# A fused layer-norm, graph and aggregation kernel: 14 pairs of batches multiplied by the weight in stage 1 in place of 8

## Chip, cores and metric

One core of one Trainium2 chip. The metric is the device time of one execution in microseconds (us). The kernel before took 948.14 us, the median of three runs (946.9 to 948.69).

## What is computed

x is 64 batches of 128 x 1024 numbers (f32), the weight ("adj") 128 x 128, the bias 128 numbers, gumbel 1024 x 1024 x 2. Cut to what matters:

```python
h = relu(layernorm(x, axis=-1))                    # rstd and shift of each row
xp = transpose(h, (2, 0, 1))                       # n=1024 nodes, 64 batches, 128
x_avg = xp.mean(axis=1); x_norm = x_avg / norm(x_avg)
sim = (x_norm @ x_norm.T + 1) * 0.5
adj = (sim + gumbel[:, 0] > 1 - sim + gumbel[:, 1])
nmask = clip(adj + adj.T + eye, 0, 1)
common = nmask @ nmask.T
W = adj * where(valid, common**2 / common.max(), 0)
Wn = dinv[:, None] * W * dinv[None, :]             # dinv = column sums ** -0.5
xw = einsum('nbt,to->nbo', xp, weight)
out = x + transpose(einsum('sd,sbt->dbt', Wn, xw) + bias, (1, 2, 0))
```

## The kernel before

The 64 batches are 32 pairs. Only after all of x has been read is the graph known, so the kernel reads x twice, and multiplies by Wn last.

**Stage 1** (to some 112 us of the span). SyncE loads the two batches of pair p into one of 8 places of xin (L316 to L321), and waits first until ScalarE has read the pair eight before. VectorE takes the statistics (long_step, L708, four instructions a pair), in groups of two pairs (GROUPS, L35), and turns those of one group into rstd and shift between the statistics of the next (L731 to L743). ScalarE takes the root that this needs (std, L481), applies norm and relu (relu, L487, two instructions a pair, into one of 4 places of h1), and copies products out of PSUM (keep, L499). The sum of h over all batches is shared: GpSimd adds the first batch of each pair to hsum (L433 to L436), TensorE adds the second through an identity into PSUM banks 0 and 1 (L1106 to L1112; of the last pair both batches). For 8 pairs, SPILLED, TensorE also multiplies the two batches by the weight (keep_product, L1097) into banks 2, 3 and 4, 5; a product may start once the copy of the same batch of the pair kept before is out. The 16 products stay in bmem (kept, L96).

**After x.** SyncE's queue has four loads of gumbel (1 MB each, load_gumbel, L326), the stores of the first four kept pairs to DRAM (spill_group, L311) between them, four more loads of gumbel, each behind a threshold, then the other four stores. Thresholds, gumbel 1 minus gumbel 0, take the place of kept products in bmem: VectorE makes rows 0 to 3 (threshold, L770), GpSimd rows 4 to 7 (L439). Row 0 stands ahead of the last addition to hsum (L776 to L780) in VectorE's order. TensorE takes two of four late batches times the weight (L1119, L1136), then sums of the squares over columns, VectorE from them the norms (L784), TensorE the 1024 x 1024 similarity row by row (L1148), VectorE compares it with the thresholds (L854). Transposes, counts of common neighbours and column sums follow. 

**Scaling and quad 0.** TensorE replicates the scale of the columns in banks 1 and 2 (L1131), ScalarE copies both to SBUF (L599 to L601), VectorE multiplies each half row of the graph by it (scaled, L907) and makes the differences that the multiplication wants (inner_of, L919).

**The quads.** Wn times xw is done for two pairs at a time, 16 quads (L1294 on), by two nested levels of seven products in place of eight: 7 slots of 28 matrix instructions in four banks each; the sums of the inputs are VectorE's (inner_sums, outer_sums), those of the outputs VectorE's, ScalarE's and GpSimd's (finish, add_kept, finish_kept; finish_here on GpSimd, L456). Quad 0 holds the two last pairs; quads 2 to 5 (LOADED) load the 8 kept pairs back from DRAM (L388 to L394). The other pairs are read from x again (load_h), put through norm and relu by ScalarE (relu_of, L534), multiplied in half batches of four matrix products ("chunks", weigh, L1235) and copied out by ScalarE (L587). This work is spread over the quad before by PLACES (L48): 12 chunks in quad 0 (for quad 1 and half of quad 6, called EXTRA; that half goes through DRAM, L407), 4 in quad 5, 8 in each of the quads 6 to 14; 88 in all. Of the chunks of quad 0, two come before the replication, four after it (FIRST_CHUNKS), six after slot 1. ScalarE's part of this, in its order: weigh(0, BEFORE), the two copies of the column scale, weigh(0, AFTER), where the third relu stands between the copies of chunks 3 and 4. Slot 0 may start once the first six are copied (L1277).

Semaphores order everything between engines; each engine runs its own list in order.

## Time and profile before

| | |
|---|---|
| median of three runs | 948.14 us |
| the profiled execution's own time | 950.07 us |
| its span | 948.2 us |
| busy: TensorE, VectorE, ScalarE, GpSimd | 909.9, 725.0, 352.1, 215.2 us |
| chain that ended last | 82% TensorE, 9% VectorE, 6% ScalarE |
| matrix products of the quads (L1311) | 690.4 us |
| chunks (L1246) | 91.8 us |
| products kept in stage 1 and the late ones (L1089) | 320 instructions |
| read from and written to DRAM | 108.07 and 42.99 MB |

Times in rows are microseconds from the span's start unless marked ns. PE is TensorE, PEld its weight loads, DVE VectorE, ACT ScalarE, POOL GpSimd, SP or SPq SyncE and its queue. A row of a timeline gives start, length, engine, line of the kernel, operation, what it writes and reads, how many instructions it merges, and in brackets the idle time before it with what ended it; the length of a merged row runs from the first start to the last end. Successive instructions overlap a little, so that the distance of two starts is shorter than a length. The profiled execution's own time is 1.9 us longer than its span.

### The profile page before, as it was taken

To read this page: it belongs to the slowest core of one execution; us is meant where nothing else is said; L and a number is where in the kernel's file an instruction comes from. 1 tells how busy PE (TensorE), PEld (TensorE's weight loads), DVE (VectorE), ACT (ScalarE), POOL (GpSimd) and SP (SyncE) were. 2 spreads that over 40 slices of the span, in tenths; PEclk is the share of its full clock that TensorE was granted. 3 is DMA by queue.
4 is the path that set the end of the run, shared out by engine and by line. 5 is a ranking of instruction groups with operands and counts; after the bars stand their busy time and mean duration, and the time that the engine had idled before them with its cause. 6 is when DMAs were issued, how large, how long until landed. Compare 5 with 4: busy or idle time off the path is not lost.

```text
span 948.2 us, 12421 instructions
## 1 busy us (share of the span) xinstructions
PE 909.9 (96%) x4603; PEld 770.4 (81%) x4607; DVE 725.0 (76%) x1492; ACT 352.1 (37%) x565; POOL 215.2 (23%) x178
## 2 busy tenths in 40 slices
PE   3899999798999999999999999999999999999997
PEld 2655565787888888888888988888889888888886
DVE  7899568999978879786858676758586766767687
ACT  4799818542212121223233423342424342424130
POOL 3588533102211111130201111111111111111111
PEclk9899999999999999999999999999999999999999
DMA  9999981321706244361524333241524242424022
GB/s 361 350 347 376 389 316 59 156 89 45 260 25 249 86 181 141 125 199 67 176 91 149 118 115 153 94 173 67 192 76 178 89 178 89 178 76 169 34 101 89
DMA packets 37485, 151.88 MB, mean 160 GB/s; under 512 B 3376, under 2 KB 3504, under 8 KB 34224
## 3 DMA queue, kind: packets, MB, share of 16 engines
q1 hardware_dynamic: 37424, 151.07, 43.3%
q8 instruction: 37, 0.61, 0.2%
q14 instruction: 24, 0.20, 0.1%
HBM read 108.07 MB, written 42.99 MB: 159 GB/s over the span
## 4 chain that ended last, share of the span: by engine, by line
PE 82%; DVE 9%; ACT 6%; issue 2%; DMA 0%; DVEq 0%; ACTq 0%
PE ps L1311 67%; PE ps L1246 7%; ACT main L495 4%; DVE bmem L915 3%; DVE stats L712 2%; PE ps L1089 2%; PE ps L1167 2%; PE ps L1148 1%; ACT bmem L502 1%; DVE bmem L908 1%; PE ps L1108 1%; PE ps L1224 1%; DVE main L1026 0%; DVE bmem L927 0%; ACT half_std L484 0%
## 5 line engine op out<-in xcount | busy, mean ns | idle before, releaser
L1311 PE MATMUL ps<-bmem,main 128*128 128x256 f32 x3136 | 690.4, 379 | 7.4 <-DVE main L993 3.8
L1311 PEld LDWEIGHTS ps<-bmem,main 128*128 128x128 f32 x3136 | 589.7, 190 | 85.2 <-issue 5.5
L463 POOL TENSOR_TENSOR main<-main 128x256 f32<-128x256 f32 x32 | 27.5, 859 | 533.0 <-ACT main L621 477.2
L993 DVE TENSOR_TENSOR main<-ps,main 128x512 f32<-128x512 f32 x124 | 76.5, 623 | 82.4 <-PE ps L1311 82.4
L593 ACT ACTIVATE main<-ps 128x512 f32<-128x512 f32 x88 | 52.3, 597 | 199.9 <-PE ps L1246 199.9
L1002 DVE TENSOR_TENSOR main<-main 128x256 f32<-128x256 f32 (+1 forms) x256 | 119.4, 539 | 0.0
L453 POOL TENSOR_TENSOR main<-main 128x256 f32<-128x256 f32 (+1 forms) x96 | 92.1, 985 | 118.9 <-DVE main L986 118.9
L1246 PEld LDWEIGHTS ps<-w_sb,main 128*128 128x128 f32 x704 | 91.2, 191 | 4.8 <-ACT main L537 0.6
L1246 PE MATMUL ps<-w_sb,main 128*128 128x128 f32 x704 | 91.8, 275 | 0.5 <-issue 0.5
L833 DVE TENSOR_TENSOR main<-main 128x256 f32<-128x256 f32 x112 | 47.0, 420 | 53.8 <-PE ps L1311 50.6
L712 DVE BATCH_NORM_STATS2 stats<-main 128x6 f32<-128x512 f32 x128 | 81.0, 672 | 4.6 <-DMA main<-in_x 4.6
L1108 PE MATMUL ps<-main,ident 128*128 128x512 f32 x132 | 67.0, 638 | 17.1 <-ACT main L495 17.1
L585 ACT ACTIVATE ps<-ps 128x512 f32<-128x512 f32 x64 | 33.8, 528 | 128.4 <-PE ps L1311 128.4
L436 POOL TENSOR_TENSOR main<-main 128x1024 f32<-128x1024 f32 x31 | 73.4, 2369 | 34.7 <-ACT main L495 33.0
L495 ACT ACTIVATE main<-main,shift,rstd 128x1024 f32<-128x1024 f32 x64 | 74.6, 1237 | 3.7 <-DVE shift L698 3.4
L585 ACT ACTIVATE main<-ps 128x512 f32<-128x512 f32 (+1 forms) x96 | 50.6, 527 | 64.7 <-PE ps L1311 64.6
L841 DVE TENSOR_TENSOR main<-main 128x256 f32<-128x256 f32 x112 | 62.6, 559 | 3.8
L1108 PEld LDWEIGHTS ps<-main,ident 128*128 128x128 f32 x132 | 24.3, 202 | 47.0 <-issue 34.9
L835 DVE TENSOR_TENSOR main<-main 128x256 f32<-128x256 f32 x112 | 55.8, 498 | 0.0
L838 DVE TENSOR_TENSOR main<-main 128x256 f32<-128x256 f32 x112 | 55.2, 493 | 0.0
L537 ACT ACTIVATE main<-main,shift,rstd 128x1024 f32<-128x1024 f32 x44 | 54.0, 1232 | 2.5 <-DMA main<-in_x 2.5
L1089 PEld LDWEIGHTS ps<-w_sb,main 128*128 128x128 f32 x320 | 40.3, 199 | 13.0 <-issue 8.1
(98 smaller groups left out, 534.9 us busy)
## 6 DMA issues: line engine op xcount, KB each, us to landing
main<-in_x SPq DMA_DIRECT2D x108, 512.0 KB, 5.6
main<-in_x SPq DMA_DIRECT2D x32, 1024.0 KB, 7.0
out<-main SPq DMA_DIRECT2D x31, 1024.0 KB, 4.9
main<-spill SPq DMA_DIRECT2D x9, 1024.0 KB, 6.9
bmem<-in_L_gnn_gumbel SPq DMA_DIRECT2D x8, 1024.0 KB, 8.9
spill<-bmem SPq DMA_DIRECT2D x8, 1024.0 KB, 13.5
spill<-main SPq DMA_DIRECT2D x2, 512.0 KB, 2.9
out<-main SPq DMA_DIRECT2D x1, 512.0 KB, 4.9
```

The lines of the kernel that those rows point to most:

```text
L436: pool.tensor_tensor(hsum[:, :], hsum[:, :], h1[:, p % HPAIRS, 0, :], ALU.add).then_inc(s_even, 1)
L453: pool.tensor_tensor(out_, out_, in_, ALU.add).then_inc(s_pool, 1)
L495: act.activation(h1[:, p % HPAIRS, b, :], xin[:, p % XPAIRS, b, :], ACT.Relu, bias=shift[:, n:n + 1], scale=rstd[:, n:n + 1]).then_inc(s_h, 1)
L585: act.activation(to, from_, ACT.Copy).then_inc(s, 1)
L712: return dve.bn_stats(stats[:, t % 2, c // 2, 6 * f:6 * f + 6], xin[:, p % XPAIRS, b, half(f)])
L841: dve.tensor_tensor(s4, q[0, 1], s2, ALU.subtract).then_inc(s_comb, 1)
L993: dve.tensor_tensor(at, piece(slot, b), at, ALU.add).then_inc(s, 1)
L1002: dve.tensor_tensor(out_, out_, in_, ALU.add).then_inc(s_low, 1)
L1089: last = pe.matmul(ps[:, first_bank + c // 4, blk(c % 4)], h[:, blk(c)], w_sb[:, :], start=True, stop=True)
L1108: last = pe.matmul(ps[:, f, :], ident[:, :], h1[:, p % HPAIRS, b, half(f)], start=p == 0, stop=True, skip_group_check=True)
L1246: last = pe.matmul(ps[:, chunk_bank(quad, k), blk(c)], hbuf[:, j % HSLOTS, blk(KC * (k % 2) + c)], w_sb[:, :], start=True, stop=True)
L1311: last = pe.matmul(piece(slot, b)[:, QUARTER * e:QUARTER * (e + 1)], left_[:, blk(c)], right_[:, c, :], start=slot in FRESH and b < 3 and ...
```

## The change

SPILLED has 14 pairs in place of 8, so quads 2 to 8 are loaded and the chunks of 12 batches are gone from the quads. The kept products have 24 places, of which 16 to 23 lie where gumbel is loaded; HOMES gives each product's place, and the first four places are used a second time by the last four products. The stores of kept pairs 0 and 1 are issued between the reads of x; four more go ahead of the first gumbel, the next four between the first gumbels, the last four behind gumbel. The last kept pair is copied by VectorE. Of six pairs (BOTH) GpSimd adds both batches to hsum, and it adds the first batch of the last pair. VectorE's chain for rstd and shift moves forward by two statistics. VectorE reads the first half of the column scale from PSUM, and ScalarE copies it later, behind the second half and two chunks. GpSimd's first sums of quad 0 wait for VectorE's last inner sums, and in quad 0 finish(0, 1) and two parts of add_kept stand before finish_kept.

```diff
-    SPILLED = [1, 3, *range(5, PAIRS - 3, 4)]
-    AHEAD = [0, 2]
+    SPILLED = [0, 1, 3, 5, 7, 9, 11, 13, 15, 17, 19, 21, 23, 25]
+    AHEAD = [2, 4]
+
+    SPILLED_EARLY = [18, 20]
+    HOMES = [*range(8, 12), *range(16, 24), *range(8), *range(12, 16), *range(8, 12)]
...
+    BOTH = range(4, PAIRS - 4, 4)
...
-    BEFORE, AFTER = (-1, 0), (-1, 1)
-    FIRST_CHUNKS = (BEFORE,) * 2 + (AFTER,) * 4 + ((1, 3),) * 6
+    BEFORE, AFTER, LATER = (-1, 0), (-1, 1), (-1, 2)
+    FIRST_CHUNKS = (BEFORE,) * 2 + (AFTER,) * 2 + (LATER,) * 2 + ((1, 3),) * 6
...
+        def spill_below(i):
+
+            return max(g for g in range(KEPT // 2) if HOMES[2 * g] <= i <= HOMES[2 * g] + 1)
+
+        LAST_SPILLS = sorted({spill_below(i) for i in range(C, 2 * C)})
...
-        SINGLE = 3
+        SINGLE = 2
...
+                if p in SPILLED_EARLY:
+                    spill_group(SPILLED_EARLY.index(p))
...
-            for i in range(0, GSLOTS, 2):
+            for k in range(C, C + KC):
+                spill_group(spill_below(2 * k))
+            for i in range(GSLOTS):
+                sp.wait_ge(s_spill[spill_below(2 * C + 2 * min(i + 1, KC - 1))], 16)
                 load_gumbel(i)
-                load_gumbel(i + 1)
-                spill_group(i)
-                spill_group(i + 1)
+                if i % 2:
+                    spill_group(spill_below(2 * i - 2))
+                    spill_group(spill_below(2 * i))
             for i in range(GSLOTS, C):
                 sp.wait_ge(s_above, i - GSLOTS + 1)
                 load_gumbel(i)
-            for g in range(GSLOTS, KEPT // 2):
+            for g in LAST_SPILLS:
                 spill_group(g)
...
-            for p in range(PAIRS - 1):
-                pool.wait_ge(s_h, 2 * p + 1)
-                wait(pool, s_even, p)
-                pool.tensor_tensor(hsum[:, :], hsum[:, :], h1[:, p % HPAIRS, 0, :], ALU.add).then_inc(s_even, 1)
+            for p in range(PAIRS):
+                for b in range(2 if p in BOTH else 1):
+                    pool.wait_ge(s_h, 2 * p + b + 1)
+                    wait(pool, s_even, evens(p - 1) + b)
+                    pool.tensor_tensor(hsum[:, :], hsum[:, :], h1[:, p % HPAIRS, b, :], ALU.add).then_inc(s_even, 1)
...
-            pool.wait_ge(s_inner, 7)
+            pool.wait_ge(s_comb, 28)
...
-                    if p == pairs[0] and t != 1 and t + 1 < len(GROUPS):
+                    if p == pairs[-1 if t < 3 else 0] and t + 1 < len(GROUPS):
                         std(t + 1)
...
-                    if p - 3 in SPILLED[:2]:
-                        keep(p - 3, 0)
+                    if p - 3 in SPILLED[:-1]:
                         keep(p - 3, 1)
+                    if p - 2 in SPILLED[:-1]:
+                        keep(p - 2, 0)
...
             weigh(0, BEFORE)
-            for f in range(2):
-                act.wait_ge(s_rep, 3 + f)
-                act.activation(columns[:, half(f)], ps[:, 1 + f, :], ACT.Copy).then_inc(s_repc, 1)
+            act.wait_ge(s_rep, 4)
+            act.activation(columns[:, half(1)], ps[:, 2, :], ACT.Copy).then_inc(s_repc, 1)
             weigh(0, AFTER)
+            act.wait_ge(s_scaled, KC)
+            act.activation(columns[:, half(0)], ps[:, 1, :], ACT.Copy).then_inc(s_repc, 1)
+            weigh(0, LATER)
...
                     aggregate(t)
+                    for b in range(2):
+                        n = KEPT - 2 + b
+                        dve.wait_ge(s_hw, n + 1)
+                        dve.wait_ge(s_spill[HOMES.index(HOMES[n]) // 2], 16)
+                        dve.tensor_copy(kept[:, HOMES[n], :], bank(2 + 2 * b, 2)).then_inc(s_kept_last, 1)
                     whole_chain(t)
                 else:
-                    long_step(t, 0)
-                    long_step(t, 1)
...
+                    for c, between in enumerate((aggregate, invert, quotient, newton, set_rstd, set_shift)):
+                        long_step(t, c)
                         if t > 3:
                             between(t - 1)
+                    long_step(t, 6)
                     long_step(t, 7).then_inc(s_bn, 1)
...
-            dve.wait_ge(s_repc, 1)
+            dve.wait_ge(s_rep, 3)
             for i in range(KC):
-                scaled(i, 0)
-            for g in range(GSLOTS, KEPT // 2):
+                scaled(i, 0, ps[:, 1, :])
+            for g in LAST_SPILLS:
                 dve.wait_ge(s_spill[g], 16)
             inner_of(0)
+            dve.wait_ge(s_repc, 2)
             for i in range(KC, C):
-                scaled(i, 0)
+                scaled(i, 0, columns[:, half(0)])
             inner_of(1)
-            dve.wait_ge(s_repc, 2)
...
+                if quad == 0:
+                    finish(quad, 1)
+                    add_kept(quad, 6, u_keep, s_ukeep, s_g21, range(2))
                 finish_kept(quad, 1, v_keep, s_g22, 16 * quad + (0 if quad + 1 < QUADS else 8))
-                finish(quad, 1)
+                if quad:
+                    finish(quad, 1)
                 if quad + 1 < QUADS:
-                    add_kept(quad, 6, u_keep, s_ukeep, s_g21)
+                    add_kept(quad, 6, u_keep, s_ukeep, s_g21, range(4) if quad else range(2, 4))
...
-                for b in ((0, 1) if p == PAIRS - 1 else (1,)):
+                if p not in BOTH:
                     for f in range(2):
...
+                if p - 1 in SPILLED:
+                    keep_product(p - 1, 1)
                 if p in SPILLED:
                     keep_product(p, 0)
-                if p - 1 in SPILLED:
-                    keep_product(p - 1, 1)
...
             weigh(0, AFTER)
+            weigh(0, LATER)
             pe.wait_ge(s_repc, 2)
```

## Rows read from the trace of the kernel before

**Rows 1.** The page: busy time of each engine over the span

```profile
PE 909.9 (96%) x4603; PEld 770.4 (81%) x4607; DVE 725.0 (76%) x1492; ACT 352.1 (37%) x565; POOL 215.2 (23%) x178
```

**Rows 2.** The chain that ended last: start, us, what; two of its pieces

```profile
239.31 172.91 PE ps L1311 x800
412.21 0.89 PE ps L1246 x8
```

**Rows 3.** Windows: one quad without chunks, busy time of each engine

```profile
324.40:366.70 42.30, 42.30 (x197) 37.24 (x196) 34.97 (x67) 8.27 (x18) 7.54 (x8) 1.00 0.42 150
```

**Rows 4.** Timeline of ScalarE, stage 1: relu, root, copy of a product

```profile
32.72 2.37 ACT L495 ACTIVATE main<-main,shift,rstd 128x1024 f32<-128x1024 f32 x2
...
55.43 0.28 ACT L484 ACTIVATE half_std<-mv,eps_sb 128x4 f32<-128x4 f32 x1
55.62 1.00 ACT L502 ACTIVATE bmem<-ps 128x1024 f32<-128x1024 f32 x1
56.52 4.63 ACT L495 ACTIVATE main<-main,shift,rstd 128x1024 f32<-128x1024 f32 x4
...
107.14 4.65 ACT L495 ACTIVATE main<-main,shift,rstd 128x1024 f32<-128x1024 f32 x4
```

**Rows 5.** Timeline of VectorE, stage 1: the shift that pair 5 waits for

```profile
32.19 0.14 DVE L698 SCALAR_TENSOR_TENSOR shift<-mv,ps 128x4 f32<-128x4 f32 x1
```

**Rows 6.** Timeline of TensorE, stage 1 and its end

```profile
31.97 3.78 PE L1089 MATMUL ps<-w_sb,main 128*128 128x128 f32 x16 [3.56 <-ACT bmem L502]
...
111.84 3.70 PE L1108 MATMUL ps<-main,ident 128*128 128x512 f32 x8 [0.28 <-ACT main L495]
115.38 3.73 PE L1089 MATMUL ps<-w_sb,main 128*128 128x128 f32 x32
```

**Rows 7.** Timeline of GpSimd, stage 1: two additions to hsum

```profile
102.84 4.86 POOL L436 TENSOR_TENSOR main<-main 128x1024 f32<-128x1024 f32 x2 [0.74 <-ACT main L495]
```

**Rows 8.** Timeline of SyncE's queue: the last eight loads of x

```profile
80.28 9.36 SPq L320 DMA_DIRECT2D main<-in_x  x8
```

**Rows 9.** DMA of 89 to 116 us: gumbel and spills after x

```profile
DMA packets 1753, 11.00 MB, mean 408 GB/s; under 512 B 190, under 2 KB 190, under 8 KB 632
```

**Rows 10.** Windows: us, PE, PEld, DVE, ACT, POOL busy, PEclk, DMA share, GB/s

```profile
80.00:90.00 10.00, 9.72 (x41) 5.43 (x40) 9.81 (x33) 10.00 (x12) 8.62 (x4) 1.00 0.99 373
```

**Rows 11.** Timeline of VectorE: norms, comparisons, scaling, end of quad 0

```profile
120.83 0.17 DVE L784 TENSOR_SCALAR node<-ps 128x8 f32<-128x8 f32 x1 [2.29 <-PE ps L1125]
...
126.74 1.22 DVE L854 TENSOR_TENSOR main<-ps,bmem 128x1024 bf16<-128x1024 f32 x1 [0.16 <-PE ps L1148]
...
138.76 1.22 DVE L854 TENSOR_TENSOR main<-ps,bmem 128x1024 bf16<-128x1024 f32 x1 [0.49 <-PE ps L1148]
...
179.46 2.74 DVE L908 SCALAR_TENSOR_TENSOR bmem<-bmem,node,main 128x512 f32<-128x512 f32 x4 [0.62 <-ACT main L601]
...
185.00 2.73 DVE L908 SCALAR_TENSOR_TENSOR bmem<-bmem,node,main 128x512 f32<-128x512 f32 x4
...
219.72 0.42 DVE L835 TENSOR_TENSOR main<-main 128x256 f32<-128x256 f32 x1
...
225.90 0.95 DVE L835 TENSOR_TENSOR main<-main 128x256 f32<-128x256 f32 x1
...
228.50 2.20 DVE L993 TENSOR_TENSOR main<-ps,main 128x512 f32<-128x512 f32 x4
```

**Rows 12.** Timeline of ScalarE between the replication and quad 0

```profile
178.76 1.13 ACT L601 ACTIVATE main<-ps 128x512 f32<-128x512 f32 x2
...
184.21 1.24 ACT L537 ACTIVATE main<-main,shift,rstd 128x1024 f32<-128x1024 f32 x1 [2.54 <-DMA main<-in_x]
```

**Rows 13.** Timeline of TensorE in quad 0

```profile
186.56 12.32 PE L1311 MATMUL ps<-bmem,main 128*128 128x256 f32 x56 [3.62 <-ACT main L593]
...
230.75 7.17 PE L1311 MATMUL ps<-bmem,main 128*128 128x256 f32 x32 [2.40 <-DVE main L993]
239.31 50.96 PE L1311 MATMUL ps<-bmem,main 128*128 128x256 f32 x235 [1.38 <-DVE main L993]
```

More of the change, by code:

```diff
@@ L207, in gnn_kernel @@
         s_kept = sem("s_kept")
+        s_kept_last = sem("s_kept_last")
         s_late_hw = sem("s_late_hw")
@@ L272, in gnn_kernel, with evens, odds @@
         block = ctx.enter_context(nc.Block())
+        def evens(p):
+            return p + 1 + sum(q <= p for q in BOTH)
+        def odds(p):
+            return p + 1 - sum(q <= p for q in BOTH)
         def wait(eng, s, value):
@@ L311, in spill_group @@
             def spill_group(g):
-                sp.wait_ge(s_kept, 2 * g + 2)
-                sp.dma_start(spill[g, :, :], kept[:, 2 * g:2 * g + 2, :].rearrange("p k n -> p (k n)")
+                if g == KEPT // 2 - 1:
+                    sp.wait_ge(s_kept_last, 2)
+                else:
+                    sp.wait_ge(s_kept, 2 * g + 2)
+                at = HOMES[2 * g]
+                sp.dma_start(spill[g, :, :], kept[:, at:at + 2, :].rearrange("p k n -> p (k n)")
                              ).then_inc(s_spill[g], 16)
@@ L488, in relu @@
                 act.wait_ge(s_row, GROUP_OF[p] + 1)
-                wait(act, s_even, p - HPAIRS + 1)
-                wait(act, s_odd, p - HPAIRS + 1)
+                wait(act, s_even, evens(p - HPAIRS) if p >= HPAIRS else 0)
+                wait(act, s_odd, odds(p - HPAIRS) if p >= HPAIRS else 0)
                 if p - HPAIRS in SPILLED:
@@ L501, in keep @@
                 act.wait_ge(s_hw, n + 1)
-                act.activation(kept[:, n, :], bank(2 + 2 * b, 2), ACT.Copy).then_inc(s_kept, 1)
+                if HOMES[n] in HOMES[0:n]:
+                    act.wait_ge(s_spill[HOMES.index(HOMES[n]) // 2], 16)
+                act.activation(kept[:, HOMES[n], :], bank(2 + 2 * b, 2), ACT.Copy).then_inc(s_kept, 1)
             std(0)
@@ L776, in _ @@
             threshold(0)
-            dve.wait_ge(s_even, PAIRS - 1)
+            dve.wait_ge(s_even, evens(PAIRS - 1))
             for f in range(2):
-                dve.wait_ge(s_last_half if f == 0 else s_odd, PAIRS if f else 1)
+                dve.wait_ge(s_last_half if f == 0 else s_odd, odds(PAIRS - 1) if f else 1)
                 dve.tensor_tensor(hsum[:, half(f)], ps[:, f, :], hsum[:, half(f)], ALU.add).then_inc(s_sum, 1)
@@ L986, in finish, with add_kept @@
                 dve.tensor_tensor(low, twice(seven), low, ALU.add).then_inc(s_fin, 1)
-            def add_kept(quad, slot, to, copied, s):
-                for b in range(4):
+            def add_kept(quad, slot, to, copied, s, banks=range(4)):
+                for b in banks:
                     at = to[:, HALF * b:HALF * b + (QUARTER if b == 3 else HALF)]
```

36 lines of the change are left out of this document (12 added, 24 removed).

## Prediction, made before the changed kernel was run

> **What bounds the kernel now.** I read the page first: TensorE is busy 96% of the span [rows 1]. The chain of waits says what that means: from 239.3 us it is nothing but matrix products of the quads and chunks, 800 products in 172.9 us without a break, then chunks of 0.89 us between them [rows 2]. A window of one quad without chunks shows TensorE busy all of its 42.3 us while VectorE works 35.0, ScalarE 8.3 and the DMA engines 42% [rows 3]. So behind 239 us the time is TensorE's instruction count. Ahead of it the bound moves. In stage 1 ScalarE has no idle time from 50 us on: one group is a root, a copy and four relus, from 55.43 to 61.06, thus 5.62 us, of which the copy takes 0.90 to the next start and the four relus and the root the rest, 1.13 us a relu [rows 4]. Its last relu ends at 111.8. Then come sums, norms, comparisons and scaling, in which TensorE and VectorE hand work to each other.
>
> **Chunks removed.** 12 batches less are multiplied in the quads: 24 chunks of 0.89 us [rows 2], -21.4 us. Quads 5, 6 and 7 lose 4, 8 and 8, quad 8 has 4 in place of 8. They become quads as in [rows 3]: 35.0 us of VectorE and 42% DMA under 42.3 us of TensorE is the cover for the 1 MB loads that replace x loads. TensorE never stops in such a quad, so the whole of a removed chunk is time.
>
> **ScalarE in stage 1.** It copies 26 products in place of 16; VectorE copies the last two. Four of the 26 fall before pair 5, where ScalarE has idle time (it waits for statistics), 22 behind, where there were 14. Pair 5's relu waits for its shift, set at 32.2 [rows 5]. The root for it now stands behind relu 4 and three copies, at about 29.1 us by my count; VectorE needs four statistics steps and small ones after it, some 3 us, so again 32.3, against 32.7 before [rows 4]: -0.3. From there 54 relus, 22 copies and 13 roots without a wait are 61.2 + 19.9 + 2.5 = 83.6, end at 116.0. The same sum for before, 14 copies, gives 109.1 where the row says 111.8: 2.3 us were waits for the third and fourth copy's products, which came late because TensorE had idled 3.56 us and did 16 products in 3.78 [rows 6], twice the 1.8 of later ones (32 take 3.73 [rows 6]). With a product in each early pair TensorE has no such gap. I add 0.1 for handshakes: the last relu ends 4.3 us later, at 116.1.
>
> **Who else could hold ScalarE.** Per two groups it now has 2 x (5.62 + 0.90) = 13.1 us. TensorE has three sums of 1.7 (8 instructions, 3.70 with the tail, are two [rows 6]) and four batches of 1.8: 12.4. GpSimd has five additions of 2.43 [rows 7]: 12.2. VectorE's eight statistics and small ones took at most the 5.62 of a group and have 6.5. DMA delivered 373 GB/s [rows 10] and now needs 2.1 MB per 6.5 us, 322 GB/s, so the two early stores, 2.6 us of DMA each, are charged nothing. Their waits on the queue were met long before; if the cover failed, each would put 2.6 us on x.
>
> **End of stage 1.** TensorE sums one batch of the last pair, not two: -1.7. GpSimd, two additions per 4.7 us at the end, trails and finishes some 1.8 us behind the last relu; VectorE then adds the halves until about 119.5, still ahead of TensorE, which needs two late products of 3.6 us before the column sums. VectorE's two copies from PSUM are priced at 1.2 each, like the comparison from PSUM [rows 11]; they end some 0.7 before relu 31 would need its shift. Norms, and all that hangs on them, come 4.3 - 1.7 = 2.6 us later than 120.83 [rows 11].
>
> **The DMA queue.** The last x load is issued when relu 23 ends: at 89.3 before (80.28 + 9.36, less the length of an issue [rows 8]), at 93.6 now (116.1 less 16 relus, 4 copies, 4 roots). Before the last threshold now stand 8 stores and 8 gumbel loads of 1.05 MB, 16.8 MB with 1.1 MB of x in flight. At the 408 GB/s of 89 to 116 us [rows 9] that is 43.9 us: gumbel 7 is there at 137.5 to 139, GpSimd's threshold takes 2.4, so 140 to 141.4. The comparison of row 7 began at 138.76 [rows 11] and would now at 141.4. No margin: I charge 0.5. Ends: 0 below; above, at the 373 GB/s of [rows 10], 48.0 us, so 144 to 145.5, +4.1. Threshold 0 needs seven transfers, 115.6, and ends just as GpSimd's last addition does; thresholds 1 to 3 fit before or beside the norms.
>
> The Trainium skill, DMA: Bandwidth & Descriptors, "Where 436 GB/s comes from", holds that for HBM to SBUF transfers the HBM's share of about 358 GB/s per core binds. By that the 17.9 MB would take 50 us and the last comparison would be some 5 us late, as an estimate from that page; the sum would then be 4 us higher. The 408 GB/s over 27 us, stores among them, disagree [rows 9].
>
> **Scaling.** VectorE can start at about 178.9 in old time, not 179.46 [rows 11], since it skips ScalarE's copy. But the copy of the same half now stands behind the third relu, which waits for its x until 184.21 and ends at 185.35 [rows 12]; the copy ends at 185.95, and VectorE's second four, begun at 185.00 [rows 11], cannot start before 186.0: +1.0. What is queued behind this wait is all of quad 0's preparation. Chunks 4 and 5 are copied 0.6 later, so slot 0 starts at 187.1, not 186.56 [rows 13]; slot 2 then starts 0.5 to 1.0 later too.
>
> **Quad 0.** GpSimd's first sums no longer run beside the last inner sums, 0.95 us where undisturbed ones are 0.42 [rows 11]: three of them, -1.45. add_kept(0, 4) thus starts at 228.5 + 1.0 - 1.45 = 228.05 and ends at 230.3, and TensorE goes on at 230.3, not 230.75: -0.45. Its next stop, 1.38 us before quad 1 [rows 13], goes away, because add_kept(0, 6) no longer stands behind 3.5 us of finish_kept: -1.4. The next to be late would be its third bank, due at 241 and ready at 240. Together -1.8.
>
> **The sum.** -21.4 + 4.3 - 1.7 + 0.5 - 1.8 = -20.1. Against the profiled execution's own 950.07 that is 930.0; the median of the runs is 1.9 lower, 948.14, and I predict that: 928.0.
>
> **Rivals.**
> - TensorE or GpSimd holds stage 1, not ScalarE: both are 93 to 95% full, and a wait of 0.3 us in each pair would cost 11 groups x 0.6 = 6.6: 934.6, or, half as bad, 931. For: small margins. Against: PSUM has a second pair of banks, h1 four places. 14%.
> - DMA holds the last comparison, +3.6 over my charge: 931.6. For: no margin. Against: 408 GB/s. 14%.
> - The third relu's x comes earlier and the scaling does not stop, and the queue costs nothing: -2.1 to -3, 925.5. Against: 2 MB of residual loads ahead of it stay there. 12%.
> - The change doesn't do what it says: loaded quads cost more than [rows 3], or half of the saving is given back in quads 5 to 8 by late loads: 938. Against: quads 1 to 4 are such quads. 3%.
> - Slower: DMA cannot sustain stores and loads mixed with x done. Place: threshold 7, before the last comparison. It decides from where 20.6 us are lost there, 17.9 MB in 65 us, 273 GB/s; at 250 GB/s 71.6 us, last comparison at 167.6, time 954. Against: nothing near this with a full queue. 2%.
> - The forecast, 55%.
>
> **Chances.** A measurement of this kernel tells about 0.2%, 2 us, from no change. Only the rival called slower ends on the other side, and the measured side is certain wherever a case is over 2 us off: faster 0.97, same 0.01, slower 0.02. The range is from 924.0 (forecast less the 2.1 us of waits and 1.5 for my count of stage 1's start, with a little more) to 934.0 (+4.1 of DMA, or most of the first rival, and the same 1.5 for the start); it leaves out 934.6, 938 and 954.
>
> **What would show it.** Right: last relu at 115 to 117; groups 6.5 us apart with no idle in ScalarE; norms at 123 to 124; comparisons 1.72 us apart with at most a short wait for gumbel on the last; VectorE idle 1 to 1.6 us before its second scaling of four; TensorE without a stop from the middle of slot 5 of quad 0; 64 chunks; quads 1 to 7 of 42.3 us each. Wrong: ScalarE waiting for TensorE in stage 1, gaps in the comparisons, any idle time of TensorE behind quad 1.

## The result and the profile after

The changed kernel took 931.11 us (median of 4 runs, 929.29 to 931.82), the kernel before 948.28 (4 runs, 946.90 to 948.69) beside it: a ratio of 0.982 [0.980, 0.984]. The forecast was 928.0, its range 924.0 to 934.0. The profiled execution of the changed kernel took 931.82 us with a span of 930.1; against the span of before, 948.2, that is 18.1 us less, where the sum said 20.1.

The page of the changed kernel, busy time of each engine, answers to [rows 1]; the second line is its rate of DRAM traffic:

```profile
PE 896.3 (96%) x4575; PEld 765.2 (82%) x4579; DVE 729.0 (78%) x1494; ACT 333.2 (36%) x539; POOL 231.0 (25%) x185
...
HBM read 108.07 MB, written 49.28 MB: 169 GB/s over the span
```

TensorE is still busy 96% of the span, but of a span 18 us shorter. 6.3 MB more are written, the six additional spills. The chain that ended last shows where quad 1 goes on (it answers to [rows 2]), and the groups of TensorE from 246 to 928 us what happens behind it (columns: instructions | busy, mean ns | idle before, releaser):

```profile
246.02 296.39 PE ps L1345 x1372
```

```profile
L1345 PE MATMUL ps<-bmem,main 128*128 128x256 f32 x2924 | 640.0, 379 | 0.9 <-DVE main L1021 0.9
L1279 PE MATMUL ps<-w_sb,main 128*128 128x128 f32 x416 | 54.8, 275 | 0.0
```

The stretch without chunks is 296.4 us long in place of 172.9, and TensorE has no idle time in it or behind it; the 0.9 us is the stop just before 246.02. All the rest happens ahead of quad 1. Stage 1 on ScalarE (timeline; start, length), for [rows 4]:

```profile
31.71 2.37 ACT L525 ACTIVATE main<-main,shift,rstd 128x1024 f32<-128x1024 f32 x2 [2.03 <-DVE shift L727]
...
53.57 0.30 ACT L514 ACTIVATE half_std<-mv,eps_sb 128x4 f32<-128x4 f32 x1
53.76 1.02 ACT L534 ACTIVATE bmem<-ps 128x1024 f32<-128x1024 f32 x1
54.66 2.38 ACT L525 ACTIVATE main<-main,shift,rstd 128x1024 f32<-128x1024 f32 x2
56.93 1.02 ACT L534 ACTIVATE bmem<-ps 128x1024 f32<-128x1024 f32 x1
57.83 2.39 ACT L525 ACTIVATE main<-main,shift,rstd 128x1024 f32<-128x1024 f32 x2
60.10 0.31 ACT L514 ACTIVATE half_std<-mv,eps_sb 128x4 f32<-128x4 f32 x1
...
110.69 4.70 ACT L525 ACTIVATE main<-main,shift,rstd 128x1024 f32<-128x1024 f32 x4
```

A group with two copies takes 6.53 us (53.57 to 60.10) and ScalarE waits for nobody; its last relu ends at 115.39, 3.6 us later than before. The path from there to the comparisons does not go through ScalarE, however. The chain of waits of 88 to 147 us:

```profile
93.99 0.20 SPq L337
...
95.11 15.48 DMA spill<-bmem
...
110.61 13.11 DMA bmem<-in_L_gnn_gumbel
...
123.81 1.23 DVE bmem L801
...
126.78 3.78 PE ps L1163 x16
130.56 14.19 PE ps L1181 x32
```

It is 28.6 us of two transfers: a store of a kept pair, issued at 95.1, which lands at 110.6, and the load of gumbel into its place, which SyncE issues only then and VectorE's third threshold waits for. VectorE's timeline shows the same from the waiting side, for [rows 11]:

```profile
118.92 1.22 DVE L801 TENSOR_TENSOR bmem<-bmem 128x1024 f32<-128x1024 f32 x1 [6.39 <-DMA spill<-bmem]
...
123.81 1.23 DVE L801 TENSOR_TENSOR bmem<-bmem 128x1024 f32<-128x1024 f32 x1 [1.33 <-DMA bmem<-in_L_gnn_gumbel]
124.95 0.16 DVE L812 TENSOR_SCALAR node<-ps 128x8 f32<-128x8 f32 x1
...
132.84 1.23 DVE L882 TENSOR_TENSOR main<-ps,bmem 128x1024 bf16<-128x1024 f32 x1 [0.42 <-PE ps L1181]
...
144.86 1.23 DVE L882 TENSOR_TENSOR main<-ps,bmem 128x1024 bf16<-128x1024 f32 x1 [0.49 <-PE ps L1181]
```

Norms begin 4.1 us later than before (124.95 against 120.83), the first and the last comparison 6.1 us later. The other 2.0 us lie between norms and first comparison, 7.89 us in place of 5.91: the replication took 3.78 us. In the windows (us, busy PE, PEld, DVE, ACT, POOL, PEclk, DMA share, GB/s) its granted clock is seen, 0.50, the lower of the two levels, 1.2 GHz. It fell between 124 and 125 us; in the 10 us before, TensorE had stopped for 0.28 and 0.47 us, and its stop of 0.87 us ahead of the replication, from 125.9, came only after the fall:

```profile
95.00:105.00 10.00, 9.73 (x59) 7.23 (x58) 8.69 (x30) 10.00 (x12) 9.38 (x4) 1.00 0.92 369
105.00:115.00 10.00, 9.25 (x32) 4.19 (x30) 6.04 (x19) 10.00 (x11) 9.43 (x5) 1.00 0.96 349
115.00:125.00 10.00, 9.25 (x66) 7.94 (x66) 4.74 (x6) 2.53 (x4) 2.47 (x2) 0.98 1.02 430
125.00:130.00 5.00, 4.13 (x20) 3.83 (x19) 3.34 (x16) 2.04 (x3) 0.00 (x0) 0.50 1.00 415
```

The same windows show the queue's hole: 349 to 369 GB/s from 95 to 115 us, 430 behind it. SyncE's timeline has four stores and then nothing to issue for 9 us, since the first gumbel waits for the second of them to land, and the third and fourth gumbel for the last of them:

```profile
93.28 3.50 SPq L337 DMA_DIRECT2D spill<-bmem  x4
105.75 2.86 SPq L353 DMA_DIRECT2D bmem<-in_L_gnn_gumbel  x2
```

Narrower windows show that the hole has two parts:

```profile
94.00:97.00 3.00, 3.00 (x20) 2.27 (x18) 3.00 (x9) 3.00 (x4) 2.35 (x2) 1.00 0.68 193
97.00:105.00 8.00, 7.73 (x44) 5.48 (x43) 6.69 (x24) 8.00 (x10) 7.57 (x4) 1.00 1.02 423
107.00:114.00 7.00, 6.25 (x14) 2.22 (x13) 5.32 (x15) 7.00 (x8) 6.57 (x4) 1.00 0.96 325
```

The rate was low while the last x loads ran out and the four stores were being issued, full while SyncE stood still, and low again when the stores had landed and the gumbels followed one by one. Against 425 GB/s each part is worth about 1.6 us, an estimate from these rates. The second part is the chain of completions; what made the first isn't shown.

GpSimd's timeline shows the end of that queue, the last two of its four thresholds. They come 2.47 us apart, each started by its gumbel:

```profile
139.87 1.89 POOL L472 TENSOR_TENSOR bmem<-bmem 128x1024 f32<-128x1024 f32 x1 [0.54 <-DMA bmem<-in_L_gnn_gumbel]
142.34 1.89 POOL L472 TENSOR_TENSOR bmem<-bmem 128x1024 f32<-128x1024 f32 x1 [0.58 <-DMA bmem<-in_L_gnn_gumbel]
```

The last one ends at 144.23. Had the clock not fallen, the last comparison would have been ready at 142.9 and would have waited until some 144.3. So of the 6.1 us 0.6 are the clock's, and 5.5 are where the queue put the last comparison. Not all of these are the queue's loss: in the kernel with all stores early, below, nothing holds that comparison and it is still 2.4 us later than before (141.20 against 138.76), by ScalarE's longer stage 1.

Last, quad 0: the four adds into the bank that TensorE waits for, finish_kept, and TensorE's stops (timelines of VectorE and TensorE, for [rows 11, 13]; TensorE's is shown up to 250 us, which shortens its last row):

```profile
231.91 0.42 DVE L869 TENSOR_TENSOR main<-main 128x256 f32<-128x256 f32 x1
232.25 2.21 DVE L1021 TENSOR_TENSOR main<-ps,main 128x512 f32<-128x512 f32 x4
...
234.71 1.49 DVE L863 TENSOR_TENSOR main<-main 128x256 f32<-128x256 f32 x1
...
240.49 4.87 DVE L1030 TENSOR_TENSOR main<-main 128x256 f32<-128x256 f32 x8
245.29 1.00 DVE L1021 TENSOR_TENSOR main<-ps,main 128x512 f32<-128x512 f32 x2
```

```profile
234.51 10.63 PE L1345 MATMUL ps<-bmem,main 128*128 128x256 f32 x48 [1.13 <-DVE main L1021]
246.02 4.15 PE L1345 MATMUL ps<-bmem,main 128*128 128x256 f32 x18 [0.88 <-DVE main L1021]
```

TensorE goes on once at 234.51 and, 16 products into quad 1, stops a second time, for the third bank, 0.88 us. Those 16 took 3.46 us, so quad 1 began at what would be 242.56 without that stop.

### The profile page after: what moved, and what is told of

Same layout as the page of the kernel before. It is cut to its first block, busy times and chain, and to the rows that moved or that the text cites. A ratio compares the mean times of both kernels' runs of the same rounds, so it can differ in the third digit from the quotient of the medians.

```text
span 930.1 us, 12349 instructions
## 1 busy us (share of the span) xinstructions
PE 896.3 (96%) x4575; PEld 765.2 (82%) x4579; DVE 729.0 (78%) x1494; ACT 333.2 (36%) x539; POOL 231.0 (25%) x185
## 4 chain that ended last, share of the span: by engine, by line
PE 77%; DVE 11%; ACT 7%; DMA 3%; issue 1%; SPq 0%; ACTq 0%; DVEq 0%
PE ps L1345 68%; ACT main L525 5%; PE ps L1279 5%; DVE bmem L943 3%; ACT bmem L534 2%; PE ps L1200 2%; DMA spill<-bmem 2%; DVE stats L741 2%; PE ps L1181 2%; DMA bmem<-in_L_gnn_gumbel 1%; DVE bmem L936 1%; DVE bmem L909 1%; DVE main L1054 0%; DVE main L1030 0%; DVE bmem L955 0%
## 5 line engine op out<-in xcount | busy, mean ns | idle before, releaser
L1021 DVE TENSOR_TENSOR main<-ps,main 128x512 f32<-128x512 f32 x124 | 76.5, 622 | 73.6 <-PE ps L1345 73.6
L1030 DVE TENSOR_TENSOR main<-main 128x256 f32<-128x256 f32 (+1 forms) x256 | 123.3, 551 | 0.0
L466 POOL TENSOR_TENSOR main<-main 128x1024 f32<-128x1024 f32 x38 | 89.9, 2365 | 24.8 <-ACT main L525 21.1
L620 ACT ACTIVATE main<-ps 128x512 f32<-128x512 f32 x64 | 37.8, 596 | 138.7 <-PE ps L1279 138.7
L525 ACT ACTIVATE main<-main,shift,rstd 128x1024 f32<-128x1024 f32 x64 | 76.2, 1263 | 4.5 <-DVE shift L727 4.5
L1121 PEld LDWEIGHTS ps<-w_sb,main 128*128 128x128 f32 x512 | 62.1, 194 | 13.5 <-issue 12.5
L1279 PEld LDWEIGHTS ps<-w_sb,main 128*128 128x128 f32 x512 | 66.0, 191 | 3.6 <-ACT main L564 0.6
L1279 PE MATMUL ps<-w_sb,main 128*128 128x128 f32 x512 | 66.5, 275 | 0.5 <-issue 0.5
L1140 PE MATMUL ps<-main,ident 128*128 128x512 f32 x104 | 51.9, 623 | 15.3 <-ACT main L525 15.0
L1121 PE MATMUL ps<-w_sb,main 128*128 128x128 f32 x512 | 63.4, 278 | 0.9 <-ACT bmem L534 0.3
L648 ACT ACTIVATE main<-ps,bias_sb 128x256 f32<-128x256 f32 x32 | 15.1, 471 | 86.1 <-PE ps L1345 72.7
```

The costliest lines, as they stand in the source:

```text
L466: pool.tensor_tensor(hsum[:, :], hsum[:, :], h1[:, p % HPAIRS, b, :], ALU.add).then_inc(s_even, 1)
L525: act.activation(h1[:, p % HPAIRS, b, :], xin[:, p % XPAIRS, b, :], ACT.Relu, bias=shift[:, n:n + 1], scale=rstd[:, n:n + 1]).then_inc(s_h, 1)
L1021: dve.tensor_tensor(at, piece(slot, b), at, ALU.add).then_inc(s, 1)
L1030: dve.tensor_tensor(out_, out_, in_, ALU.add).then_inc(s_low, 1)
L1121: last = pe.matmul(ps[:, first_bank + c // 4, blk(c % 4)], h[:, blk(c)], w_sb[:, :], start=True, stop=True)
L1279: last = pe.matmul(ps[:, chunk_bank(quad, k), blk(c)], hbuf[:, j % HSLOTS, blk(KC * (k % 2) + c)], w_sb[:, :], start=True, stop=True)
```

## The experiments

The theory after this result: the removed chunks gave exactly what was forecast, and the 2 us that are missing lie ahead of quad 1, above all in the queue of stores and gumbel loads; rivals are the thresholds that stand in VectorE's path to the norms, the granted clock, and ScalarE's longer stage 1. All edits are to the changed kernel. The experiments timed only once are named as such.

**Thresholds later.** Thresholds 0 and 1 stand behind the additions to hsum, 2 and 3 behind its scaling.

```diff
-            threshold(0)
             dve.wait_ge(s_even, evens(PAIRS - 1))
...
-            threshold(1)
-            threshold(2)
+            threshold(0)
+            threshold(1)
             dve.wait_ge(s_col, 1)
...
+            threshold(2)
             threshold(3)
```

> The changed kernel with VectorE's thresholds moved: 0 behind the additions to hsum, 1 after it, 2 and 3 behind the scaling of hsum. Theory A (DMA decides: from 93 us on sixteen 1 MB transfers must pass before the eighth threshold, and GpSimd's four thresholds each waited for gumbel at 135 to 142 us): the norms come at about 123 us in place of 124.95 and the first comparison some 3 us earlier, but the last comparison still starts at 144.5 to 145, and the time stays within 0.7 us of the changed kernel's 931.1. Theory B (VectorE's waits for spill and gumbel and the clock drop that follows them are the loss): the last comparison starts about 3 us earlier, at 141.5 to 142, and the time is 928.

931.36 us (928.51 to 931.80), ratio 0.982 [0.980, 0.984]: no change of the median. Its profiled execution, the fastest of the four, shows what holds the end. VectorE's timeline, last two comparisons:

```profile
139.30 1.22 DVE L882 TENSOR_TENSOR main<-ps,bmem 128x1024 bf16<-128x1024 f32 x1 [0.49 <-PE ps L1181]
141.63 1.23 DVE L882 TENSOR_TENSOR main<-ps,bmem 128x1024 bf16<-128x1024 f32 x1 [1.10 <-POOL bmem L472]
```

The first comparison ran at 129.90, 2.9 us sooner, and the last one then waited for GpSimd's threshold, which waited for gumbel. The gumbels themselves came 2.6 us sooner in this execution, which this edit does not explain. By its time and its last comparison this one execution would fit Theory B; the unedited kernel, run again below, has the same two numbers in its good executions (927.8 and 141.07), so they need not be the edit's.

**All six stores early.** Four more pairs are stored between the reads of x, none ahead of gumbel.

```diff
-    SPILLED_EARLY = [18, 20]
+    SPILLED_EARLY = [18, 20, 22, 24, 26, 28]
...
-            for k in range(C, C + KC):
-                spill_group(spill_below(2 * k))
```

> The changed kernel with four more stores of kept pairs (the third to the sixth) issued between the reads of x instead of behind them. Theory A: 4.2 MB of the queue and the hole in it at 107 to 113 us go away; threshold 0 no longer waits, norms at 122.5 to 123.5 us, GpSimd's thresholds ready on time, last comparison at 141 to 142, time 927 to 928. TensorE's granted clock stays at 1.00 from 120 to 135 us. Rival: the early stores take DMA time from x, VectorE waits for x in stage 1 and the last relu ends later than 116 us, so that nothing or little is gained (930 to 932).

928.82 us (928.01 to 930.26), ratio 0.980 [0.978, 0.982]. The hole is gone (windows), and with it every wait for gumbel in the comparisons (VectorE's last one; lines are two lower in this kernel):

```profile
95.00:105.00 10.00, 9.69 (x58) 7.21 (x57) 8.43 (x30) 9.66 (x11) 9.27 (x4) 1.00 1.03 420
105.00:115.00 10.00, 9.11 (x32) 4.40 (x31) 8.33 (x21) 10.00 (x12) 9.31 (x5) 1.00 1.01 428
```

```profile
141.20 1.22 DVE L880 TENSOR_TENSOR main<-ps,bmem 128x1024 bf16<-128x1024 f32 x1 [0.49 <-PE ps L1179]
```

The edit takes the hole away and also four stores, 4.2 MB, from behind x, so by itself it doesn't tell order from bytes. The rates of the changed kernel do, as an estimate: from 93 to 137 us it moved 17.1 MB at a mean of 389 GB/s; at the 426 of 115 to 140 us the 17.9 MB of the forecast would be through 4 us sooner than at 389, GpSimd's last threshold would end at about 140.2, and the last comparison, at 141.20 here, would not wait for it. Stage 1 paid little: ScalarE was busy 9.66 of 10 us in the first window, and its last relu ended at 115.95, 0.6 later than in the changed kernel.

**A filler for TensorE.** One batch more is multiplied before the late products, so that TensorE does not rest before the replication.

```diff
             column_sums(6)
+            times_weight(h1[:, (PAIRS - 1) % HPAIRS, 0, :], 0)
             late_times_weight(2, 0)
```

> The changed kernel with one more weight product of a late batch (1.8 us, thrown away) on TensorE between the column sums and the replication. It fills the idle time at 125.9 us. If the idle time is what lowered the clock, the granted clock stays at 1.00 from 125 to 135 us, the replication takes 2.05 us in place of 3.78, and the first comparison starts about 2 us earlier, at 131. Theory A: the last comparison is still held by gumbel, at 144.5 or later, and the time is unchanged (931, within 0.7). Theory B: 929.

930.92 us (929.76 to 931.09), ratio 0.982 [0.980, 0.983]. In its profile the clock was 1.00 from 120 to 135 us, the replication took 1.95 us, the first comparison ran at 130.61, 2.2 us sooner than in the changed kernel's profile, and the last at 142.94 after 0.81 us of waiting for GpSimd's threshold. It came sooner than the 144.5 of Theory A, since the last gumbel was 1.3 us sooner in this execution. That the filler held the clock isn't shown: in the first profile the clock fell before 125 us, while TensorE was still multiplying by the weight as it did here, and the filler adds work only behind 125.9. Without a filler the clock was 1.00 from 125 to 130 us in every other profile but that of 24 batches (0.94), once after stops of 0.27 and 1.39 us (the order of quad 0 undone).

**Both of the first two edits.**

> Both edits together: thresholds moved on VectorE and four more stores between the reads of x. Theory A: the early stores alone remove all waits, so this is the same as e2_spills_early within 1 us, 927 to 928. Theory B (VectorE's order matters by itself): 1.5 us or more faster than e2_spills_early.

930.03 us (928.60 to 931.55), ratio 0.981 [0.979, 0.983], no better than the early stores alone (928.82). Two thresholds that now ran beside GpSimd's took 4.05 us in place of 2.35 and put the first comparison at 132.36, against 129.18 with early stores alone. So moving the thresholds gains nothing even where the queue is full.

**GpSimd's gate undone** (one run each for this and the next). GpSimd's first sums of quad 0 may again run beside VectorE's last inner sums.

```diff
-pool.wait_ge(s_comb, 28)
+pool.wait_ge(s_inner, 7)
```

> The changed kernel with GpSimd's first sums of quad 0 let go after the seventh inner difference again, as before the change. Theory A: GpSimd slows VectorE by the same amount wherever its four sums fall; VectorE's last inner sums take 1.45 us longer (0.95 us where they now take 0.42), but finish_kept and the inner sums of quad 1 become shorter by as much (finish_kept 3.5 in place of 4.87 us), so TensorE's last stop, for the third bank in quad 1, ends at the same time within 0.5 us. Rival, my term of the forecast: the gate is worth its 1.45 us, and quad 1 starts that much later without it.

930.99 us. Counted from the start of VectorE's second scaling of four, the additions (L1021) start at 43.51 us in place of 42.02, and TensorE goes on with the third bank of quad 1 at 56.75 in place of 55.79. VectorE's timeline:

```profile
229.35 0.95 DVE L863 TENSOR_TENSOR main<-main 128x256 f32<-128x256 f32 x1
230.22 0.94 DVE L866 TENSOR_TENSOR main<-main 128x256 f32<-128x256 f32 x1
231.20 0.83 DVE L869 TENSOR_TENSOR main<-main 128x256 f32<-128x256 f32 x1
231.95 2.20 DVE L1021 TENSOR_TENSOR main<-ps,main 128x512 f32<-128x512 f32 x4
...
234.41 0.95 DVE L863 TENSOR_TENSOR main<-main 128x256 f32<-128x256 f32 x1
...
239.65 4.89 DVE L1030 TENSOR_TENSOR main<-main 128x256 f32<-128x256 f32 x8
```

The gate is worth 1.49 us where it stands, as forecast (1.45), but only 0.96 at quad 1: with it VectorE's next inner sum takes 1.49 us and not 0.95, since GpSimd's sums now run beside that one. finish_kept took 4.89 us here too; that it would be shorter without the gate was wrong, so its length is not the gate's doing.

**The order of quad 0 undone.** finish_kept stands again before finish(0, 1) and add_kept(0, 6).

```diff
-                if quad == 0:
-                    finish(quad, 1)
-                    add_kept(quad, 6, u_keep, s_ukeep, s_g21, range(2))
...
-                if quad:
-                    finish(quad, 1)
+                finish(quad, 1)
                 if quad + 1 < QUADS:
-                    add_kept(quad, 6, u_keep, s_ukeep, s_g21, range(4) if quad else range(2, 4))
+                    add_kept(quad, 6, u_keep, s_ukeep, s_g21)
```

> The changed kernel with finish(0, 1) and add_kept(0, 6) behind finish_kept again. Theory A: VectorE's work up to the last piece of add_kept is the same, but TensorE needs the first bank at once: it stops ahead of quad 1's first product instead of its third, and resumes when the first of four pieces is done, some 1.3 us later than now in the terms of quad 1's start (now 3.46 us before the resumption, thus 242.6 us; then 243.9). Rival: the order is worth the whole 3.5 to 4.9 us of finish_kept.

931.1 us. TensorE's timeline:

```profile
239.14 1.13 PE L1341 MATMUL ps<-bmem,main 128*128 128x256 f32 x4 [0.57 <-DVE main L1002]
241.88 10.38 PE L1341 MATMUL ps<-bmem,main 128*128 128x256 f32 x47 [1.61 <-DVE main L1021]
```

Quad 1 starts 53.93 us behind the second scaling (187.95 to 241.88), in the changed kernel 52.33 (190.23 to 242.56): the order is worth 1.60 us, where 1.4 was forecast. In that sum the stop for the third bank is already taken off. finish_kept took 4.10 us in this order. In the new one it takes 4.87, beside GpSimd's sums for finish(0, 1), which have been released by then.

**ScalarE copies the last pair** (one run each for this and the next); VectorE's two copies go.

```diff
-                        dve.tensor_copy(kept[:, HOMES[n], :], bank(2 + 2 * b, 2)).then_inc(s_kept_last, 1)
...
-                if p - 3 in SPILLED[:-1]:
+                if p - 3 in SPILLED:
```

> The changed kernel with the last kept pair copied by ScalarE as the others, not by VectorE. The last relu ends 1.8 us later (two copies of 0.9), at about 117.2 us. Theory A (behind stage 1 the DMA queue decides, not ScalarE): VectorE waits for the spill of threshold 0 until about 118.9 us as now, the norms and the last comparison move by at most 0.7 us. Rival (ScalarE's stage 1 sets the time): everything behind moves by 1.8 us.

930.85 us. The last relu ended at 116.94, 1.55 us later than in the changed kernel; norms ran at 124.26 and the last comparison at 142.18, no later than in the first profile of the changed kernel. Threshold 0 waited for its store until 117.95, and GpSimd's last threshold ended at 142.10, so here the queue and ScalarE's path ended together: the later end of ScalarE cost at most 0.1 us. Against the second profile of the changed kernel, below, where that threshold ended at 141.03, the last comparison is 1.1 us later; behind such a queue ScalarE would have been the bound.

**The same with all stores early.**

> The same edit on the kernel of e2_spills_early, where nothing waits for the queue. Theory A: now the 1.8 us are paid in full: last relu at 117.8 us, norms at 125, last comparison at 143 against 141.2 in e2_spills_early.

929.93 us. Against the early stores alone, the last relu ends at 117.73 in place of 115.95 (+1.78), norms run at 125.06 in place of 123.28 (+1.78), the last comparison at 142.97 in place of 141.20 (+1.77), and the two profiled executions differ by as much (929.93 against 928.20). Behind a full queue ScalarE is the bound, and its 1.78 us were paid in full.

**24 batches in stage 1 in place of 28**, in 24 places, none used twice, and no early store.

```diff
-    SPILLED = [0, 1, 3, 5, 7, 9, 11, 13, 15, 17, 19, 21, 23, 25]
-    SPILLED_EARLY = [18, 20]
-    HOMES = [*range(8, 12), *range(16, 24), *range(8), *range(12, 16), *range(8, 12)]
+    SPILLED = [0, 1, 3, 5, 7, 9, 11, 13, 15, 17, 19, 21]
+    SPILLED_EARLY = []
+    HOMES = [*range(16, 24), *range(16)]
...
-                        dve.wait_ge(s_spill[HOMES.index(HOMES[n]) // 2], 16)
```

> The changed kernel with 24 batches kept (pairs 23 and 25 are not), no place used twice, and no store between the reads of x. Each pair not kept puts 4 chunks of 0.89 us back into the quads, +7.1 us for two pairs, and takes two copies of 0.9 us from ScalarE's stage 1, -3.6 us for two. If the chain behind stage 1 starts that much earlier, the time is 931.1 + 3.5 = 934.6. Rival: the queue, which still has sixteen transfers to pass before the last comparison, gives nothing back, and the time is 937 to 938.

936.50 us (935.45 to 937.71), ratio 0.988 [0.986, 0.989]: 5.4 us slower than the changed kernel (8.3 than its second measurement, below), where 8 chunks more are 7.1 us. The median lies between the two expected times, 934.6 and 937, and with 3 us between the two measurements of the changed kernel it doesn't decide; the trace does. ScalarE ended 2.4 us sooner, at 112.95, and that was not seen at the norms (123.93), since VectorE's timeline has the same wait, only longer:

```profile
117.80 1.23 DVE L800 TENSOR_TENSOR bmem<-bmem 128x1024 f32<-128x1024 f32 x1 [7.72 <-DMA spill<-bmem]
```

The queue behind x has the same 16 transfers ahead of the last threshold, and the last comparison, at 142.00, again began just behind the end of that threshold, 141.96.

**The changed kernel again**, unedited, on the chip of the next two:

> The changed kernel itself, unedited, for comparison on the same chip: 930 to 932. The clock drop at 125 to 130 us was seen in one profile only of the kernels with this stage; if it is an accident of the execution, this profile has the norms at 123.5 to 124.7, the clock at 1.00 there, and the last comparison at 141.5 to 143, held by the fourth threshold of GpSimd, which waits for gumbel.

928.15 us (927.30 to 931.67), ratio 0.980 [0.978, 0.981] to 948.08 of before (9 runs). The median is 3 us below that of the first measurement; whether the chip or the execution does it isn't shown. The profiled execution (927.8, span 926.1) is one of the good ones; SyncE's first gumbels, VectorE's norms and its last comparison (timelines):

```profile
103.45 2.83 SPq L353 DMA_DIRECT2D bmem<-in_L_gnn_gumbel  x2
```

```profile
122.39 0.16 DVE L812 TENSOR_SCALAR node<-ps 128x8 f32<-128x8 f32 x1
...
141.07 1.23 DVE L882 TENSOR_TENSOR main<-ps,bmem 128x1024 bf16<-128x1024 f32 x1 [1.19 <-POOL bmem L472]
```

The first gumbel was issued 2.3 us sooner, DMA ran at 394 and 411 GB/s from 95 to 115 us, and the last comparison came 3.8 us sooner, still held by gumbel, by 0.8 us. The clock was 1.00 at 125 to 130 us. The same program thus has a hole of varying size: 250 GB/s in place of 193 from 94 to 97 us, and 410 in place of 325 from 107 to 114.

**All stores early again**, beside it:

> The kernel of e2_spills_early again, five rounds: 1.5 to 3 us below e11_after_again, if the queue of sixteen transfers is what the changed kernel loses behind stage 1.

928.00 us (927.85 to 928.47), ratio 0.979 [0.977, 0.980]. The last comparison ran at 141.53, unheld. The median is that of the changed kernel, not 1.5 to 3 us better as expected: what the hole costs in the median is not shown on this chip, and the 2.1 to 2.5 us by which the early stores were ahead of the two edits without them (filler, later thresholds) stand on the other chip alone, where both edits together had half of it (930.03). The scatter differs here, 0.6 us over five runs against 4.4 over four, but the same kernel had 2.3 on the other chip, and the next one, with the same full queue, has 2.4 on this chip; so a full queue doesn't explain it.

**All stores early, and the third bank filled before finish_kept.**

```diff
-                    add_kept(quad, 6, u_keep, s_ukeep, s_g21, range(2))
+                    add_kept(quad, 6, u_keep, s_ukeep, s_g21, range(3))
...
-                    add_kept(quad, 6, u_keep, s_ukeep, s_g21, range(4) if quad else range(2, 4))
+                    add_kept(quad, 6, u_keep, s_ukeep, s_g21, range(4) if quad else range(3, 4))
```

> The kernel of e2_spills_early with the third piece of add_kept(0, 6) ahead of finish_kept too. TensorE's stop of 0.88 us for the third bank of quad 1 goes away or shrinks to under 0.2 us, since the fourth piece is due 1.7 us after it; the time is 0.7 to 0.9 us below e12_spills_early_again, about 927.5 to 928. Rival: the fourth bank or VectorE's next inner sums become the stop and nothing is gained.

928.24 us (926.82 to 929.23), ratio 0.979 [0.978, 0.980]. TensorE's timeline from slot 2 of quad 0 on (window to 252 us) has no stop any more (the kernel without this edit, in its profile, had only the second, 0.88 us):

```profile
207.54 44.63 PE L1343 MATMUL ps<-bmem,main 128*128 128x256 f32 x204
```

The span of the profile is 1.1 us shorter than that of the run before (925.6 against 926.7), 0.3 of it ahead of the second scaling and 0.8 behind, about the stop of 0.88; the medians do not tell the two apart.

## Why the prediction was right, and where its terms were off

The sign, the size and the range held. The sum of 20.1 came out as 18.1 between the two profiled executions; step by step:

| part | forecast | first profile | second profile |
|---|---|---|---|
| to the last comparison | +3.1 | +6.1 | +2.3 |
| from there to the second scaling | +1.0 | -0.9 | -1.1 |
| from there to quad 1 | -2.8 | -2.0 | -2.0 |
| quads and chunks | -21.4 | -21.4 | -21.3 |
| span | -20.1 | -18.1 | -22.1 |

(Second profile: the unedited kernel run again; last comparison 141.07, second scaling 186.19, quad 1 at 242.00 - 3.46 = 238.54, span 926.1. Before: 138.76, 185.00, 239.31, 948.2; that execution was 1.9 us over its median, so that the -22.1 is more than the medians on that chip differ by, 19.9.)

That the first profile comes within 2.0 us of the sum is in part luck: the last comparison was 3.0 later than forecast and quad 0 gave 0.8 less, while the scaling gave 1.9 more than forecast.

- **Chunks.** 948.2 - 239.31 = 708.9 before, 930.1 - 242.56 = 687.5 after: -21.4. The cover of [rows 3] held, and the additional spill loads cost nothing.
- **ScalarE.** Pair 5 at 31.71, forecast 32.3; groups 6.53 us apart, forecast 6.52; last relu at 115.39, forecast 116.1. The addition of 4.3 measured 3.6, because pair 5's shift came 0.6 sooner than the 32.3 of my count. No other engine held it: the first rival (14%) is out. (The prediction's own sum for before left 2.7 us over, of which it named 2.3 as waits.) With an empty path behind it this term is paid in full (+1.78 for +1.78 above).
- **The queue: the term furthest off.** "At the 408 GB/s ... that is 43.9 us", "I charge 0.5". The bytes were right; the mean rate from 93 to 137 us was 389 GB/s in the first profile and 406 in the second, with 415 to 431 from 115 us on in the first. The four stores ahead of gumbel and the gumbels behind them are a chain of completions: a store was issued at 95.1, landed at 110.6, and its gumbel landed at 123.7. That chain is the second of the two low stretches; the first, from 94 to 97 us, has no cause shown. The mean of 408 over 27 us in [rows 9] shows no hole, and I carried it over to a kernel whose stores stand differently. The last gumbel's threshold could start at 142.34 in the first profile and at 139.14 in the second; I had 137.5 to 139. In place of the 0.5 charged, the queue cost about 2.9 in the first profile (144.3 without the fall of the clock, against 141.4) and 0.8 in the second (the wait at its last comparison). The second rival named this place, with 3.6 over the charge, by a lower rate and not by a chain. The Trainium skill's rule of about 358 GB/s (DMA: Bandwidth & Descriptors, "Where 436 GB/s comes from") isn't seen in this kernel, which runs on one core: the windows have 415 to 431 GB/s from 115 us on, with stores to DRAM among the loads.
- **The norms.** Forecast 123.4, measured 124.95 and 122.39. I had threshold 0 at 115.6 and thresholds 1 to 3 "before or beside the norms". (Seven transfers and what was in flight, at 408 GB/s, are there at 114.3; the prediction doesn't say what the other 1.3 are.) In the first profile, threshold 0 waited 6.39 us for its store, until 118.92, and threshold 2 another 1.33; in the second, threshold 0 ran at 115.76. The edit with later thresholds shows that this wait by itself is worth nothing: the last gumbel sets the end. In seven of the eight profiles without the four earlier stores the last comparison began 0.03 to 0.08 us behind the end of GpSimd's last threshold; the eighth is the first profile, with its fall of the clock.
- **The clock**, forecast by no step: 2.0 us at the first comparison, 0.6 at the last, in one profile of the two. What lowered it there isn't shown, nor that the filler prevents it.
- **The scaling, +1.0.** This wait is not in either profile of the changed kernel, where ScalarE's third relu waited only 0.79 and 0.74 us for x, in place of the 2.54 of [rows 12]. It is there with 1.14 to 1.70 us (VectorE idle before L936, <-ACT L630) in four profiles: the filler, the undone gate, ScalarE's copies of the last pair, and 24 batches. Those four have a granted clock of 0.91 from 160 to 180 us, as the kernel before had; all the others have 1.00. So the wait exists, but it depends on the execution. Even with it the step is +0.1 to +0.8, not +1.0, since VectorE's first four now start 0.7 to 1.0 us sooner after the last comparison. That this wait did not come was the first half of the third rival (12%); its second half, a queue that costs nothing, did not hold. What sets the clock there isn't settled, nor which of clock and wait follows from the other.
- **Quad 0.** -2.8 came out as -2.0. Gate and order measured 1.49 and 1.60 by themselves, 1.45 and 1.4 forecast. The difference is the third bank: "due at 241 and ready at 240". In measured time the additions for it stood behind a finish_kept of 4.87 us, not 3.5, and one inner sum of quad 1 took 1.49 us, not 0.95. Each is GpSimd's work moved: the gate put its first sums beside that inner sum (without the gate 0.95, and the stop 0.36), and the new order released its sums for finish(0, 1) ahead of finish_kept (4.10 with the order undone, 4.89 with only the gate undone). The stop for the third bank was 0.88 us.
- **Signs named ahead.** Seen: the last relu, the groups, comparisons 1.72 us apart, 64 chunks, no idle time of TensorE behind that stop. Not seen: norms at 123 to 124, VectorE idle before its second scaling, and TensorE without a stop from slot 5 of quad 0 on.

The median was missed by 3.1 us: 1.8 in the sum (930.0 against the profiled 931.82), and 1.3 because I put the median 2.0 under the profiled execution as before, where that of the changed kernel lay only 0.7 over its median (931.82 against 931.11). On the other chip the kernel had 928.15, so that a hit to 0.2 us there would be luck as much as the 3.1 here is a miss: its single executions scatter from 927.3 to 931.8.

## What to carry to other kernels

A queue whose bytes are right can still be late: look in it for an issue that waits for a completion (a load into the place of a store), and lay the stores early enough that none is ahead of the loads that count. A term on a path pays only as far as the next wait lets it: ScalarE's later end (1.55 and 1.78 us) cost at most 0.1 us behind the one queue and 1.8 behind the other. And moving one engine's work away from another's in order to end contention needs an answer to the question beside what it will run instead.

## What the runs showed of the hardware

- The rate of DMA held 415 to 431 GB/s with stores and loads mixed, one 1 MB gumbel each 2.4 to 2.5 us. Where the x loads ran out and four stores of 1 MB followed, with loads that waited for them to land, it fell to 349 to 369 over 20 us in one execution, and to 394 to 411 in another of the same program.
- The same code had a granted clock of 0.50 at 125 to 130 us in one execution and 1.00 in another. In the 10 us before, TensorE was busy 9.25 us in the first and 9.91 in the second; but with the order of quad 0 undone it was busy 9.44, stopped for 1.39 us soon after, and kept 1.00. Likewise the clock was 0.91 or 1.00 from 160 to 180. Executions of one kernel on nominally equal terms are 4.4 us apart, 0.5%, more than most of the terms that were in dispute.
- VectorE's additions with both operands in SBUF lengthened beside GpSimd (0.42 to 0.95 or 1.49 us; two thresholds 2.35 to 4.05), while none of the 124 additions with an operand from PSUM (L1021) took over 0.69 us, beside GpSimd or not.
